# Fused attention and feed-forward kernel on one core: order of weight-sum transfers, down products, a late weight split and one round of weight sums

## What is computed

```python
def _L0_ffn_ref(x, w_gate, w_up, w_down):
    h = jax.nn.silu(jnp.einsum('bsh,hi->bsi', x, w_gate)) * jnp.einsum('bsh,hi->bsi', x, w_up)
    h_sparse = _sparsify_2to4(h)
    return jnp.einsum('bsi,ih->bsh', h_sparse, w_down)
x = L0_attn_x
x = x + _layernorm(_L0_attn_ref(_layernorm(x, axis=-1), L0_attn_Wq, L0_attn_Wk, L0_attn_Wv, L0_attn_Wo), axis=-1)
x = x + _layernorm(_L0_ffn_ref(_layernorm(x, axis=-1), L0_ffn_w_gate, L0_ffn_w_up, L0_ffn_w_down), axis=-1)
```

## Time and profile before

| | us |
|---|---|
| median of 3 runs | 1197.79 (1196.38 to 1200.12) |
| the profiled execution, device time | 1199.08 |
| its span in the trace | 1197.3 |
| PE busy in the span | 1167.0 |
| DVE busy | 859.1 |
| ACT busy | 520.6 |
| POOL busy | 414.2 |
| moved by DMA | 153.77 MB |

### The profile page before, as it was taken

How to read it: one execution, slowest core, us unless ns; L and a number is a source line. 1 busy time by engine, 2 the same in 40 slices (tenths; PEclk the granted TensorE clock), 3 DMA queues, 4 the chain that set the end, 5 groups by cost and what they waited for, 6 DMA issues and landing times.

```text
span 1197.3 us, 16275 instructions
## 1 busy us (share of the span) xinstructions
PE 1167.0 (97%) x5862; PEld 982.3 (82%) x5862; DVE 859.1 (72%) x1460; ACT 520.6 (43%) x1017; POOL 414.2 (35%) x349
## 2 busy tenths in 40 slices
PE   8999999999999999999999989899999999999996
PEld 7888888888888888888888878678788887888875
DVE  8944756756664456666665897878777879868788
ACT  5533454544544335455355543334433444333432
POOL 6421533515555125244245533123423342001013
PEclk9999999999999999999999999999999999999999
DMA  7221323322434114133055766667422565343421
GB/s 224 77 80 51 100 74 80 88 49 80 145 101 141 54 52 125 51 88 97 22 150 180 262 222 226 203 230 273 133 88 96 195 208 187 123 158 123 158 71 71
DMA packets 96367, 153.77 MB, mean 128 GB/s; under 512 B 10272, under 2 KB 31008, under 8 KB 96288
## 3 DMA queue, kind: packets, MB, share of 16 engines
q1 hardware_dynamic: 96288, 152.74, 41.1%
HBM read 96.60 MB, written 40.89 MB: 115 GB/s over the span
## 4 chain that ended last, share of the span: by engine, by line
PE 76%; DVE 12%; POOL 3%; ACT 2%; DMA 2%; SPq 2%; issue 2%; DVEq 0%; ACTq 0%; POOLq 0%
PE bank_q L809 8%; PE bank_q L807 8%; PE bank_q L808 8%; PE bank_y L809 5%; PE bank_y L808 5%; PE bank_y L807 5%; PE bank_od L1035 5%; PE bank_od L1038 4%; PE bank_t L807 3%; PE bank_t L809 3%; PE bank_t L808 3%; PE bank_s L932 2%; PE bank_od L807 2%; PE bank_od L808 2%; PE bank_od L809 2%; PE bank_s L807 2%
## 5 line engine op out<-in xcount | busy, mean ns | idle before, releaser
L807 PE MATMUL bank_q<-x_hi,w_hi 128*128 128x512 f32 x464 | 186.3, 402 | 0.1
L809 PE MATMUL bank_q<-x_lo,w_hi 128*128 128x512 f32 x464 | 181.6, 391 | 0.0
L808 PE MATMUL bank_q<-x_hi,w_lo 128*128 128x512 f32 x464 | 181.1, 390 | 0.0
L1937 POOL TENSOR_TENSOR w_lo<-stage,w_hi 128x512 fp32r<-128x512 f32 x60 | 81.4, 1366 | 224.9 <-ACT w_hi L1211 224.1
L1937 POOL TENSOR_TENSOR big_lo<-q_rows,big_hi 128x1024 fp32r<-128x1024 f32 x31 | 73.9, 2384 | 116.8 <-ACT big_hi L1250 116.7
L809 PEld LDWEIGHTS bank_q<-x_lo,w_hi 128*128 128x128 f32 x464 | 87.2, 188 | 18.9
L807 PEld LDWEIGHTS bank_q<-x_hi,w_hi 128*128 128x128 f32 x464 | 87.5, 189 | 17.1 <-ACT scratch L1338 0.7
L808 PEld LDWEIGHTS bank_q<-x_hi,w_lo 128*128 128x128 f32 x464 | 87.6, 189 | 16.7
L809 PE MATMUL bank_y<-wout_lo,a_hi 128*128 128x512 f32 x256 | 100.0, 391 | 0.0
L808 PE MATMUL bank_y<-wout_hi,a_lo 128*128 128x512 f32 x256 | 99.8, 390 | 0.0
L807 PE MATMUL bank_y<-wout_hi,a_hi 128*128 128x512 f32 x256 | 99.8, 390 | 0.0
(11 more groups left out here) (423 smaller groups left out, 3015.6 us busy)
## 6 DMA issues: line engine op xcount, KB each, us to landing
q_rows<-scratch SPq DMA_DIRECT2D x116, 128.0 KB, 2.4
x_rows<-x SPq DMA_DIRECT2D x40, 256.0 KB, 3.1
stage<-wq SPq DMA_DIRECT2D x32, 256.0 KB, 2.8
stage<-wo SPq DMA_DIRECT2D x32, 256.0 KB, 2.7
s_keep<-x_hi SPq DMA_DIRECT2D x16, 512.0 KB, 4.5
s_keep<-x_lo SPq DMA_DIRECT2D x16, 512.0 KB, 5.3
w_hi<-s_keep SPq DMA_DIRECT2D x32, 256.0 KB, 3.4
w_lo<-s_keep SPq DMA_DIRECT2D x32, 256.0 KB, 4.4
```

Of the source, the lines that this page charges most:

```text
L807: pe.matmul(ps, whi, xhi, start=first, stop=False, skip_group_check=True)
L808: pe.matmul(ps, wlo, xhi, start=False, stop=False, skip_group_check=True)
L809: return pe.matmul(ps, whi, xlo, start=False, stop=last, skip_group_check=True)
L1937: return pool.tensor_tensor(dst, full, hi.bitcast(F32), ALU.subtract)
```

## The change

Five edits, all of order; what is computed stays.

1. In SP's slot `store_sums` and `load_sums` stand ahead of the stores and loads of rows, the stage loads and `store_piece`.
2. `SUM_AT`: the round of slot 3 moves; slots 3 and 4 lose a round of sums and its low part, the rounds 3 to 12 come one place later in the list (round 3 in slot 5, round 4 in slot 6, and so on), and slot 16 has a round now.
3. `sum_low` stands right after the multiply in DVE's slot, ahead of the pairs and the choice.
4. `down_beat`: the last two down products of units 0, 1 and 2 go in one slot (y = 6 and 7 in slot 13, 14 and 15 in 21, 22 and 23 in 29); slots 14, 22 and 30 have none. With it the piece ("d", u, 3) is split at the head of its slot (14, 22, 30) on ACT and POOL, and stands in the plan ahead of that slot's gate and up pieces.
5. Row 7 of the first batch row is normalised one slot later (42).

The hunks below are in this order: the tables and the plan, SP (ahead of the stores of rows; behind `store_piece`), ACT and POOL (head of the slot; behind silu and the casts of hidden rows, the same on both), DVE (behind the multiply; end of the slot).

```diff
 def down_beat(y):
     if y < EDGE:
-        return y + 7 if y < EDGE - 3 else (36, 38, 40)[y - EDGE + 3]
+        return 8 * (y // 8) + 7 + min(y % 8, 6) if y < EDGE - 3 else (36, 38, 40)[y - EDGE + 3]
...
-SUM_AT = [0, 1, 2, 3, 5, 6, 7, 9, 10, 11, 12, 13, 14, 15, 17, 18]
+SUM_AT = [0, 1, 2, 5, 6, 7, 9, 10, 11, 12, 13, 14, 15, 16, 17, 18]
...
-    return tick_f(65 + t if b else add_beat(24 + t))
+    return tick_f(65 + t if b else add_beat(24 + t) + (t == TT - 1))
...
             for j in range(4):
-                plan += [(("g", u + 1, j), tick_f(8 * u + 5 + j)), (("u", u + 1, j), tick_f(8 * u + 5 + j))]
                 if j == 1 and u:
                     plan += down
+                plan += [(("g", u + 1, j), tick_f(8 * u + 5 + j)), (("u", u + 1, j), tick_f(8 * u + 5 + j))]
...
+                if kind == "f":
+                    for r in range(ROUNDS):
+                        if SUM_AT[r] + 2 == i:
+                            store_sums(r)
+                    for r in range(4, ROUNDS):
+                        if max(SUM_AT[r - 4] + 3, SUM_AT[r] - 2) == i:
+                            load_sums(r)
...
                 if kind == "f":
-                    for r in range(ROUNDS):
-                        if SUM_AT[r] + 2 == i:
-                            store_sums(r)
-                    for r in range(4, ROUNDS):
-                        if max(SUM_AT[r - 4] + 3, SUM_AT[r] - 2) == i:
-                            load_sums(r)
...
                 for k in pieces_at(tick, "d"):
-                    if not last_down(PLAN[k][0]):
-                        split(k)
+                    split(k)
...
-                for k in pieces_at(tick, "gud"):
-                    if PLAN[k][0][0] != "d" or last_down(PLAN[k][0]):
-                        split(k)
+                for k in pieces_at(tick, "gu"):
+                    split(k)
...
                 for job in at(tick - 1, lambda j: turn_tick(*j), TURNS):
                     split_x(job)
+                for r in range(ROUNDS):
+                    if SUM_AT[r] + 1 == n:
+                        sum_low(r)
...
                 for job in stats:
                     variance(job)
                 for r in range(ROUNDS):
-                    if SUM_AT[r] + 1 == n:
-                        sum_low(r)
-                for r in range(ROUNDS):
                     if SUM_AT[r] == n:
                         sum_weights(r)
```

More of the change, by code:

```diff
@@ L232 @@
 PIECE = {piece: k for k, (piece, _) in enumerate(PLAN)}
-def last_down(piece):
-    return piece[0] == "d" and piece[2] == 3
 def pieces_at(tick, kinds):
@@ L2007, in slot_f @@
                     scaling(job)
-                for k in pieces_at(tick, "gud"):
-                    if not last_down(PLAN[k][0]) and PLAN[k][0][0] == "d":
-                        continue
+                for k in pieces_at(tick, "gu"):
                     split(k)
```

## The result

| | before | after |
|---|---|---|
| median, us | 1197.79 (1196.38 to 1200.12) | 1185.23 (1184.89 to 1186.23) |
| profiled execution, us | 1199.08 | 1186.23 |
| its span | 1197.3 | 1184.4 |
| DVE idle ahead of the sums for a DMA | 21.5 us in 4 waits | none |

The ratio is 0.9895 (95% interval 0.9881 to 0.991): 1.05% faster. The forecast was 1181.5 with a range of 1178 to 1189, so the time lies in the range, 3.7 us above the point. The sum of 16.2 us was made against the profiled execution; there it is 1199.08 - 1186.23 = 12.85 us. The lines have other numbers now: the matmuls are L804 to L806, the multiply L1779, the pairs L1621 to L1623, the low parts of hidden rows (`big_lo`) L1654, the four operations of a sum L1661 to L1666, the low part of sums L1671.

A forecast was written before the change was run, and what follows sets the result against it. PE bounds the kernel, so only its idles and slow spells can help, ceiling 17.1 us. Gains 4.0 + 2.06 + 6.68 + 0.33 + 2.21 + 0.9 = 16.2 us gave 1181.5 us, range 1178 to 1189.

The forecast's parts named there:

- rival (B): DVE stays late at slot 18, so PE's gains at slots 6, 14, 15 are only lent: 1185 to 1193, chance 0.20.
- slot 18: PE's 0.33 us wait for DVE's multiply of slot 17 goes; DVE done at 792.8 or 786.9, PE wanting it at 794.0.
- Slot 6: DVE's multiply of slot 5 comes 2.4 to 3.3 us earlier; PE's stall of 3.02 and slow spell shrink, gain 4.0 us.
- caught as feared: The low part of slot 3, ahead of the pairs, blocked by POOL: up to 1.1 us more at slot 6, not summed.
- The waits for loads: DVE's 21.5 us of waits before sums shrink as loads feed a later slot; 4 us left in slot 11, 2 in 15.
- Slot 14: PE's stall of 2.06 us for DVE's multiply of slot 13 goes whole, with a margin of 6 us.
- Slots 15 and 23: PE's stalls for POOL's split of the last down piece go: 6.68 us with slow spell at 15, 2.21 at 23.
- Two down products in one slot: Costs PE nothing while DVE is ahead; 2.7 us in each of the three slots if DVE is behind.
- Slot 42: Moving row 7's variance shortens PE's 1.23 us wait for a DVE sum to 0.2 to 0.35: gain 0.9 us.
- (A): The forecast itself: all five stalls of slots 6 to 23 go but for a remainder, 1178 to 1185, chance 0.70.
- (C): SP's strict list, with stage loads behind stores and loads of sums, delays slots 16 and 24: 1201 to 1203, chance 0.05.
- (D): Edits cancel: the extra round of slot 16 pins PE at slot 18, only 2.21 + 0.9 remain: 1195, chance 0.05.

The follow-up runs named there:

- after: The changed kernel with all five edits against the kernel before: 1185.23 us, 0.9895; measured a second time at 1185.78 us, 0.9916.
- the round in slot 19: Changed kernel with the round of sums of slot 16 moved to slot 19, all else as it is: 1181.08 us, 0.9873 against the kernel before.
- loads alone ahead: Changed kernel with only the loads of sums ahead of SP's stage loads, the stores back behind `store_piece`: 1189.22 us, 0.9941 against the kernel before.
- mixed: Changed kernel with the low part of sums ahead of the pairs only in choice slots, at the slot's end elsewhere: 1181.8 us, 0.9874 against the kernel before.

## Why the prediction was right, and where it was off

**The number and the mechanism.** The time lies in the range because the range reached to the middle of rival (B). The mechanism failed at one step, slot 18 below, and 1.0 us of the 12.85 is luck: it was won in the first 12 us of the execution, before anything that was edited (an idle of PE of 1.26 us at 6.60 before, 0.30 at 5.96 after).

**What bounds the kernel.** Right: the time moved with PE's idles and slow spells, and the ceiling of 17.1 us held.

**Slot 6, 4.0 us.** 3.02 + 1.58 - 1.26 - 0.13 = 3.2 us. The net gain of DVE was put at 2.4 to 3.3. Edit 2 reached it: 0.2 to 0.4 us stay in the kernels with the new list where the sums of slot 2 get through first (0.84 in the one with the old down products). In `after` the four caught sums took 0.8 us of it, and the low part of slot 3 took 1.22 us, not caught. Where the sums got through, it was caught as feared (2.37 to 2.38 us with the round in slot 19, SP's order undone, loads alone ahead), and the idle was small all the same. The Trainium skill (SBUF — State Buffer, "Who interferes with whom") says that a VectorE operation with two SBUF inputs and a GpSimd operation that reads SBUF contend, and that issue order decides which of them blocks. DVE's rows of slot 2 agree with it: with a start of POOL 0.04 us ahead, four sums take 1.40 to 1.53 us instead of 0.42.

**The waits for loads.** Their going was right, and its cause half wrong. The prediction said that the loads "now" feed "a slot (8.2 us, three groups) later", which credits the list of rounds. With that list and the old order on SP 13.6 us of waits stay; with the old list and the new order 0.2. The order on SP does it alone. The 4 us that I left in slot 11 and the 2 in slot 15 were not there: the load for slot 11 was issued at 731.94 (forecast 731.5), but DVE asked for it at 742.34, not at 736, since its own work held it. That is the first sign of what follows.

**Slot 18, 0.33 us forecast as gained, 4.3 lost.** This is the step that failed: the sum of DVE's gains up to the multiply of slot 17. PE's side was right: it wanted the multiply at 796.17 - 2.94 = 793.2 us, 794.2 on the clock of the trace before (all starts in `after` are 1.0 us earlier from slot 5 on, by PE's start of slot 6), and 794.0 was forecast. DVE's side was put at 792.8 or 786.9 and was 795.35 + 0.68 + 1.0 = 797.0. Already the multiply of slot 12 was at 744.8 on that clock, not 740. The subtraction took the waits away and left the rest as it was. The windows show what took their place: waits for ACT's cast of 0.52 us in each of 10 rounds, where I had counted a small gain in three choices and, outside them, nothing, and 8.7 us more of busy time, 1.5 of the new round and 7.1 of operations caught by POOL, of which the sum had only the 1.5 plus a catch. Undone one by one: the new round is worth 2.4 us at the multiply of slot 17, the place of the low parts 1.9 to 2.5 (the time between the two multiplies is 101.23 us in `after`, 99.31 with all low parts at the end, 98.70 mixed). Mixed, that is all in DVE's waits (5.2 to 2.6 us); with all at the end it is 0.8 us of waits and 1.1 of busy time. Either is enough to end the slow spell, and both together end the stall.

**Slot 14, 2.06 us.** Gone whole. The margin was 2 us and not 6: DVE's multiply of slot 13 was over at 757.57 + 0.68 = 758.3, PE went on at 760.3.

**Slots 15 and 23, 6.68 and 2.21 us.** Both stalls went, as did the slow spell; the cast of `wout_hi` came at 760.7, ahead of PE's use by 7 us (asked for: 5 or more). But the credit to edit 4 was half wrong. Alone it does end both stalls, and the time stays, since PE then waits for DVE. And edit 1 alone takes the stall of slot 15 from 5.24 to 1.39 and that of slot 23 away: the piece is split behind the multiply of slot 14, and that comes 7.0 us earlier once the loads of sums are in time (766.15 instead of 773.19). In `after` edit 4 is worth 0.9923 against 0.9895, 3.3 us.

**Two down products in one slot,** priced at nothing: no idle at slots 13, 21 and 29. Right.

**Slot 42, 0.9 us.** 1.23 to 0.21 is 1.02. Every kernel with the variance of row 7 a slot later has 0.19 to 0.22 us there, those without it 1.23 or 1.24. Right.

**What the sum lacked.** 16.2 forecast and 12.85 measured: slot 6 lacks 0.8, slot 18 lacks 4.64 (the 0.33 not gained, 2.61 of new idle, 1.70 of slow spell); 1.0 came from the start of the execution, where nothing was edited, 0.1 from slot 42, and 1.0 lies in small rests (such as 0.13 us behind each short stall).

**Rivals.** The time lies at the edge between (A) and (B), and the mechanism at slot 18 is (B)'s, DVE late at its multiply, with another cause: not loads that land late but DVE's own list. (B)'s "PE's gains are only lent" is what the run with edit 4 alone shows in pure form. (C), SP held by the stores, did not come with both moved, and came in part when only the loads were ahead. (D)'s extra round was real, 2.4 us and not the whole.

## What to carry to other kernels

Taking long waits off an engine with a fixed list does not give back their length: ask how full the list is between two points that others wait for (here 86.6 us of 109.3), and how much longer its operations get when more of them run beside another engine. An operation that is moved takes its neighbours along: ask what now stands where it stood. In a strict DMA queue, a load that needs nothing but a free buffer belongs ahead of those that wait for an engine, together with the store that frees its buffer. And test edits in pairs: one that gave 0 alone gave 3.1 us on top of the one that gave 8.0.

## What the runs showed of the hardware

- **DVE beside POOL.** A sum of 128x256 in SBUF took 0.42 us alone and 1.40 to 1.53 when POOL's addition or split had begun first. Between the multiplies of slots 5 and 17 all caught rows of DVE overlap POOL: 10 before, 15 with edit 1 alone, 14 with the low parts moved but the loads late, 16 after. So catches grew both with the missing waits and with the order. I had priced them at one place each.
- **The clock behind a stall.** Behind 2.94 us of idle PE ran at a granted clock of 0.63 for 4.6 us, between the two levels of 1.2 and 2.4 GHz in the mean, and a group took 4.42 us; behind 1.26 us the first twelve took 2.85. Behind 6.22 us (order on SP undone) the twelve took 4.63, hardly more. Over all these traces no spell came behind an idle of up to 2.21 us and one came behind each of 2.78 us and more, 13 in all. It cost 1.3 to 2.5 us in the first twelve matmuls, up to 3.0 with the next twelve, and did not grow with the stall ahead of it (1.9 behind 6.22, 3.0 behind 2.78). A stall of 2.9 to 3.0 us cost some half as much again as its own length (1.5 to 1.8).
- **A steady near-tie.** Which of two engines starts first, by 0.04 us, came out the same in two traces of one kernel and the other way in three kernels that differ from it only in SP's order or 14 slots further on.
